# Moving x's transposes, the output projection and both layernorms to other units of the attention pipeline

## What is computed

```python
def layernorm(x): return (x - mean(x)) / sqrt(var(x) + 1e-5)

def attention(h):                      # 32 heads of 16 channels
    q, k, v = h @ Wq.T + bq, h @ Wk.T + bk, h @ Wv.T + bv
    q, k = apply_rope(q), apply_rope(k)          # q * cos + rotate_half(q) * sin
    scores = q @ k.T / sqrt(16)                  # causal mask, softmax over keys
    return softmax(where(causal, scores, -inf)) @ v @ Wo.T + bo

x = x + layernorm(attention(layernorm(x)))
x = x + layernorm(ffn(layernorm(x)))             # silu(x @ gate.T) * (x @ up.T) @ down.T
```

## Time and profile before

| | |
|---|---|
| median of three runs | 2859.64 us |
| profiled execution | 2851.13 us, its span 2849.4 us |
| TensorE matmul busy | 2545.8 us, 89% |
| VectorE busy | 2134.7 us, 75% |
| ScalarE busy | 1422.9 us, 50% |
| GpSimd busy | 1007.2 us, 35% |
| mean granted TensorE clock | 0.962 |
| attention phase | to about 1825 us of the span |

### The profile page before, as it was taken

How to read it: one execution, slowest core, us unless ns; L and a number is a source line. 1 busy time by engine, 2 the same in 40 slices (tenths; PEclk the granted TensorE clock), 3 DMA queues, 4 the chain that set the end, 5 groups by cost and what they waited for, 6 DMA issues and landing times. The chain is left out here.

```text
span 2849.4 us, 55752 instructions
## 1 busy us (share of the span) xinstructions
PE 2545.8 (89%) x19584; PEld 1220.5 (43%) x19584; DVE 2134.7 (75%) x6399; ACT 1422.9 (50%) x1838; POOL 1007.2 (35%) x1083
## 2 busy tenths in 40 slices
PE   4899889889898898898898997349999999999997
PEld 2444344444444443453444443114444444444443
DVE  6899889889889898898898997355455555555454
ACT  3666667666666666666666666142222222222221
POOL 4556455455455555564554563100000000000000
PEclk9999999999999999999999999669999999999999
DMA  5332332332332332333333331401111111111111
GB/s 170 94 89 76 113 111 68 113 120 66 111 117 71 108 113 73 108 101 88 111 91 91 104 104 32 197 18 45 44 59 44 69 49 44 59 44 74 44 44 45
DMA packets 125311, 236.64 MB, mean 83 GB/s; under 512 B 11440, under 2 KB 94896, under 8 KB 111920
## 3 DMA queue, kind: packets, MB, share of 16 engines
q1 hardware_dynamic: 123056, 232.84, 26.1%
q10 hardware_dynamic: 2048, 1.05, 0.1%
HBM read 148.39 MB, written 84.41 MB: 82 GB/s over the span
## 5 line engine op out<-in xcount | busy, mean ns | idle before, releaser
L650 DVE CUSTOM_DVE_ANT_0 mx<-mx,causal 128x512 f32<-128x512 f32 (+3 forms) x2048 | 944.7, 516 | 38.0 <-PE mx L779 34.7
L487 ACT ACTIVATE probs<-ts,exp_scale 128x1024 f32<-128x1024 f32 x640 | 709.5, 1109 | 421.8 <-PE ts L793 421.2
L1222 DVE SCALAR_TENSOR_TENSOR hidden<-gu,up_scale,silu 128x512 f32<-128x512 f32 x176 | 131.9, 749 | 418.7 <-PE gu L1272 418.7
L1081 ACT ACTIVATE silu<-gu,gate_scale 128x512 f32<-128x512 f32 x176 | 121.0, 688 | 632.0 <-PE gu L1272 632.0
L401 POOL TENSOR_SCALAR_AFFINE_SELECT probs<-probs 128x512 f32<-128x512 f32 x512 | 313.8, 637 | 199.9 <-ACT probs L487 199.8
L1056 POOL TENSOR_TENSOR f_rstd<-f_var,f_neg_half 128x4 f32<-128x4 f32 x32 | 32.3, 1010 | 929.6 <-DVE f_var L1199 647.2
L380 POOL TENSOR_TENSOR turned<-biased,sin_sb 64x512 f32<-64x512 f32 x128 | 172.0, 1344 | 469.5 <-ACT biased L472 469.5
L807 PE MATMUL xb<-probs,vs 128*32 128x512 f32 (+3 forms) x4096 | 308.7, 443 | 7.6 <-ACT shift_rows L493 5.6
L1270 PE MATMUL gu<-f_xT_hi,gate_hi 128*128 128x512 f16 x704 | 267.9, 381 | 52.1 <-issue 52.1
L779 PE MATMUL mx<-kT,qT 64*128 64x512 f16 (+3 forms) x2048 | 253.3, 306 | 37.8 <-DVE row_max L650 35.7
L650 DVE DVE_READ_ACCUMULATOR2_ANT row_max<- 128x1 f32 x2048 | 282.6, 138 | 0.0
(11 more groups left out here) (148 smaller groups left out, 4553.3 us busy)
## 6 DMA issues: line engine op xcount, KB each, us to landing
slots<-half SPq DMA_DIRECT2D x260, 128.0 KB, 12.5
qT<-slots SPq DMA_DIRECT2D x128, 256.0 KB, 3.8
kT<-slots SPq DMA_DIRECT2D x128, 256.0 KB, 4.0
xn<-x SPq DMA_DIRECT2D x16, 1024.0 KB, 6.8
xr<-x SPq DMA_DIRECT2D x16, 1024.0 KB, 4.9
slots<-half SPq DMA_DIRECT2D x256, 64.0 KB
x<-xr SPq DMA_DIRECT2D x16, 1024.0 KB, 5.6
f_xn<-x SPq DMA_DIRECT2D x16, 1024.0 KB, 4.8
```

Source lines behind the costliest of these rows:

```text
L487: nc.scalar.activation(probs[:, g % 2, u, :, :], ts[:, :, :], ACT.Exp, scale=exp_scale[:, 0:1]).then_inc(ts_read, 1)
L650: last = nc.vector.tensor_tensor_reduce(out=scores, in0=scores, in1=causal[:, T - P * (qt + 1):T], scale=1.0, scalar=-3e38, op0=ALU.add, o ...
```

## The change

- `TURNED`: x is transposed in groups 0, 1, 4, 6 (tiles 2, 3 of the next sequence, tiles 0, 1 of the one after), the attention output in groups 2, 3, 5, 7. Before it was x in 0, 2, 4, 6 and the attention output in 1, 3, 5, 7.
- `V_OR_OUT`: the output projection of the previous sequence in groups 3 to 6 instead of 1 to 4, v in groups 0, 1, 2 and 7 instead of 0, 5, 6, 7.
- First layernorm: load of x in unit 8, statistics in 14 and 15, variance in 15, root in 16, normalisation in 19, 20, 20, 21. Second: statistics in 21, 26, 31, 36, variance and root in 36; normalisation in 0, 1, 4, 5 and residual in 1 and 6 of the body after. x1 is stored in unit 9 of that body and xr loaded in unit 14.
- `cosine` stands behind the low half and the maxima in VectorE's list. As the low half is in unit 3 and the cosine product in unit 2, what changes is that unit 2's maxima come first.
- `aT_hi` and `aT_lo` have NC + 2 tiles. Every engine gets a `body(NB + 1)`; SP and GpSimd write out `body(1)` and loop from 2.

```diff
-        aT_hi = sb("aT_hi", [P, NC + 1, T], F16)
-        aT_lo = sb("aT_lo", [P, NC + 1, T], F16)
+        aT_hi = sb("aT_hi", [P, NC + 2, T], F16)
+        aT_lo = sb("aT_lo", [P, NC + 2, T], F16)
...
-        V_OR_OUT = (("v", 3, 0), ("out", 0, -1), ("out", 1, -1), ("out", 2, -1), ("out", 3, -1),
-                    ("v", 0, 1), ("v", 1, 1), ("v", 2, 1))
-        TURNED = (("x", 3, 1), ("a", 3, -1), ("x", 0, 2), ("a", 0, 0), ("x", 1, 2), ("a", 1, 0), ("x", 2, 2), ("a", 2, 0))
+        V_OR_OUT = (("v", 1, 0), ("v", 2, 0), ("v", 3, 0), ("out", 0, -1), ("out", 1, -1), ("out", 2, -1), ("out", 3, -1),
+                    ("v", 0, 1))
+        TURNED = (("x", 2, 1), ("x", 3, 1), ("a", 3, -1), ("a", 0, 0), ("x", 0, 2), ("a", 1, 0), ("x", 1, 2), ("a", 2, 0))
...
-        STATISTICS_AT = {5: (0, 1), 6: (2, 3)}
-        VARIANCE_AT = 6
-        ROOT_AT = 8
-        NORMALISE_AT = {10: (0, 1), 11: (2, 3)}
-        STATISTICS1_AT = {11: 0, 16: 1, 21: 2, 26: 3}
-        VARIANCE1_AT = 26
-        ROOT1_AT = 28
-        NORMALISE1_AT = {30: (0, 1), 31: (2, 3)}
-        RESIDUAL_AT = {31: (0, 1), 35: (2, 3)}
+        STATISTICS_AT = {14: (0, 1), 15: (2, 3)}
+        VARIANCE_AT = 15
+        ROOT_AT = 16
+        NORMALISE_AT = {19: (0,), 20: (1, 2), 21: (3,)}
+        STATISTICS1_AT = {21: 0, 26: 1, 31: 2, 36: 3}
+        VARIANCE1_AT = 36
+        ROOT1_AT = 36
+        NORMALISE1_AT = {0: (0,), 1: (1,), 4: (2,), 5: (3,)}
+        RESIDUAL_AT = {1: (0, 1), 6: (2, 3)}
...
-                    if s == 3 and exists(i + 2):
+                    if s == 8 and exists(i + 2):
                         sp.wait_ge(xT_full, NC * (i + 2))
                         sp.dma_start(xn[:, :, :], x[i + 2, :, :, :]).then_inc(x_in, 16)
-                    if s == 38 and exists(i - 1):
-                        sp.wait_ge(x1_ready, NT * i)
-                        sp.dma_start(x1[i - 1, :, :, :], xr[:, :, :]).then_inc(x1_out, 16)
-                    if s == 39 and exists(i - 1) and exists(i):
-                        sp.wait_ge(x1_out, 16 * i)
-                        sp.dma_start(xr[:, :, :], x[i, :, :, :]).then_inc(xr_in, 16)
+                    if s == 9 and exists(i - 2):
+                        sp.wait_ge(x1_ready, NT * (i - 1))
+                        sp.dma_start(x1[i - 2, :, :, :], xr[:, :, :]).then_inc(x1_out, 16)
+                    if s == 14 and exists(i - 2) and exists(i - 1):
+                        sp.wait_ge(x1_out, 16 * (i - 1))
+                        sp.dma_start(xr[:, :, :], x[i - 1, :, :, :]).then_inc(xr_in, 16)
...
-                    if u == 2:
-                        n, owner = QUERIES_KEYS[g]
-                        if exists(i + owner):
-                            cosine(i + owner, n)
                     if u == 3:
                         kind, c, owner = TURNED[g]
                         if in_turn(kind, i + owner):
...
                         maxima(i + ahead, n)
                         if n % NU == NU - 1:
                             shift_of_maxima(i + ahead, n // NU)
+                    if u == 2:
+                        n, owner = QUERIES_KEYS[g]
+                        if exists(i + owner):
+                            cosine(i + owner, n)
```

More of the change, by code:

```diff
@@ L328, in body @@
                         fetch_slots(i + owner, n)
-                    if s == 3 and exists(i + 2):
+                    if s == 8 and exists(i + 2):
                         sp.wait_ge(xT_full, NC * (i + 2))
                         sp.dma_start(xn[:, :, :], x[i + 2, :, :, :]).then_inc(x_in, 16)
-                    if s == 38 and exists(i - 1):
-                        sp.wait_ge(x1_ready, NT * i)
-                        sp.dma_start(x1[i - 1, :, :, :], xr[:, :, :]).then_inc(x1_out, 16)
-                    if s == 39 and exists(i - 1) and exists(i):
-                        sp.wait_ge(x1_out, 16 * i)
-                        sp.dma_start(xr[:, :, :], x[i, :, :, :]).then_inc(xr_in, 16)
+                    if s == 9 and exists(i - 2):
[4 more added lines that the diff above has]
+                        sp.dma_start(xr[:, :, :], x[i - 1, :, :, :]).then_inc(xr_in, 16)
             body(-1)
             body(0)
-            with sp.Fori(1, NB - 2) as i:
+            body(1)
+            with sp.Fori(2, NB - 2) as i:
                 body(i)
@@ L345, in _ @@
             body(NB)
+            body(NB + 1)
             sp.wait_ge(x1_out, 16 * NB)
@@ L429, in body @@
                                               minus_mean1[:, :], offset1[:, :], offset1_ready)
-                    if exists(i - 1):
+                    if exists(i - 2):
                         for t in RESIDUAL_AT.get(s, ()):
-                            before = residual(i - 1, t)
+                            before = residual(i - 2, t)
             inverse_root(0, var_ready, var[:, :], rstd[:, :], rstd_ready,
@@ L439, in _ @@
             body(0, (roped_done, 6))
-            with pool.Fori(1, NB - 2) as i:
+            body(1)
+            with pool.Fori(2, NB - 2) as i:
                 body(i)
@@ L453, in high_of_attention @@
                 act.wait_ge(aT_full, NC * i + c + 1)
-                nc.scalar.activation(aT_hi[:, (NC * i + c) % (NC + 1), :], xb[:, bank, :], ACT.Copy).then_inc(aT_hi_done, 1)
+                nc.scalar.activation(aT_hi[:, (NC * i + c) % (NC + 2), :], xb[:, bank, :], ACT.Copy).then_inc(aT_hi_done, 1)
             def normalise_x(i, t):
@@ L529, in body @@
                             normalise_x(i + 2, t)
-                    if exists(i - 1):
+                    if exists(i - 2):
                         for t in NORMALISE1_AT.get(s, ()):
-                            normalise_projected(i - 1, t)
+                            normalise_projected(i - 2, t)
             for t in range(NT):
@@ L619, in low_of_attention @@
                 dve.wait_ge(aT_hi_done, NC * i + c + 1)
-                place = (NC * i + c) % (NC + 1)
+                place = (NC * i + c) % (NC + 2)
                 nc.vector.tensor_tensor(aT_lo[:, place, :], xb[:, bank, :], aT_hi[:, place, :],
@@ L877, in project_out @@
                 for c in (2 * part, 2 * part + 1):
-                    place = (NC * seq + c) % (NC + 1)
+                    place = (NC * seq + c) % (NC + 2)
                     last = three_products(out, aT_hi[:, place, cols], aT_lo[:, place, cols], w_hi[:, 3, c, :], w_lo[:, 3, c, :],
```

## The result

The changed kernel takes 2744.84 us (median of four runs, 2744.56 to 2745.20). Run on the same chip, the kernel before takes 2861.89 (four runs, 2857.48 to 2865.51). The ratio is 0.9592, 95% interval 0.9575 to 0.9608: faster by 117 us, where 92 was forecast.

A forecast was written before the change was run, and what follows sets the result against it. TensorE and VectorE nearly fill regular groups; 11 us of each 109.25 us sequence are stalls. Sequences become 102.15, saving 85 over twelve; with neighbouring sequences and ends −92, so 2859.64 becomes about 2767, range 2722 to 2822.

The forecast's parts named there:

- Load and statistics of x: Group 1: with x loaded earlier, VectorE's 5.26 us wait, the idle time and slow clock go, 8.2 us per sequence.
- fourth rival: The x1 store behind the load makes x land after 16 us, VectorE waits again: 2830 to 2860 us; chance 0.06.
- Cosine product late: Regular groups: cosine product behind unit 2's maxima waits for GpSimd's second half, low half at +3.99; cost 0.
- Group 3: Statistics and variance of x ahead of its rotation delay the low half to +5.74: cost 1.45 per sequence, 2.8 if late.
- second rival: In group 3 the cosine product misses its gap and the clock falls: 2785 to 2835 us; chance 0.24.
- Normalisation of x: Group 4: four normalisations on ScalarE make the bias 1.12 us late, in place of the former 1.53.
- Second layernorm: Group 0 loses 0.32 instead of 1.53 to a normalisation; group 7 newly loses 1.06 to the root before its rotation.
- +4.29: Latest low-half start after a group's start that does not stall TensorE, which wants the freed bank at +5.03.
- SP and the ends: Moved x1 store, xr load and exchanged groups: 0 in regular groups; start −4 (−8 to 0), end −1 (−4 to +3).
- The offset of 8.5 us: The profiled execution of the kernel before lay 8.5 under the median; the same was expected for the changed kernel.
- the layernorms cost nothing: First rival: VectorE has room, so stretched layernorms add near 0; sequences 98.5 to 100, 2710 to 2742 us; chance 0.15.
- the other two: Rivals: low half stalls TensorE in every group, 2860 to 2900 (0.05); x still lands late, 2830 to 2860 (0.06).

The follow-up runs named there:

- e1: The kernel before without the load of x for sequences 2 to 15 (the layernorm works on what the tile holds): 2775.03 us, ratio 0.9696.
- e2: The kernel before with only the cosine product moved behind unit 2's maxima: 2857.29 us, ratio 0.9993.
- e3: The changed kernel with the cosine product back in front of unit 2's maxima: 2743.92 us, ratio 0.9588.
- e8: The changed kernel with variance and root of x moved from units 15 and 16 to unit 18: 2744.25 us, ratio 0.9587.
- e9: e6 with the load of x's separate statistics tile issued before the fetch of q or k instead of after it: 2717.05 us, ratio 0.9505.
- e4: The changed kernel with both inverse roots two units later (18 and 38), behind the rotation in GpSimd's list: 2764.54 us, ratio 0.9661.
- e10: e7 with the cosine product back in front of unit 2's maxima: 2728.10 us, ratio 0.9536.
- e5: The changed kernel with x's normalisation in units 18, 18, 19, 20 instead of 19, 20, 20, 21: 2735.43 us, ratio 0.9557.
- e7: e5 with the second layernorm's normalisations in units 3, 3, 4, 5 and residuals in 4 and 6: 2728.14 us, ratio 0.9532.
- e11: e9 with the second of x's four statistics in unit 8 instead of 6: 2714.35 us, ratio 0.9501.
- e6: e7 with one statistic of x per group, from a separately loaded tile, and SP's loop over bodies written out: 2743.18 us, ratio 0.9581.

## Why the prediction was right, and where not

Forecast 2767 in a range of 2722 to 2822, measured 2744.84. The sign and the main mechanism hold; the gain was 25 us larger than forecast, and the near agreement of the twelve sequences (85 forecast, 94 measured) holds errors both ways. Point by point:

1. **Load and statistics of x (−8.2 a sequence).** Right: group 1 takes 12.31 at a clock of 1.00, and the median of e1 falls by 85 us with the transfer alone. The fourth rival's mechanism, the x1 store behind the load, is seen in small: the median landing of x rose from 6.8 to 9.1. The longest, 9.7, was no longer than the 10.1 that the text reckoned with, and in the tightest sequence (body 11) x landed 4.5 before VectorE reached its statistics. The instructions on xn, in the changed kernel:

```profile
DMA to landing us min/median/max: 4.8/9.1/9.7
```

2. **Cosine product late (0).** Right: it starts at +2.36 and lasts 1.69 in a v group, low half at +3.98 against +3.99 worked out; e2 and e3 confirm the zero for regular groups.
3. **Group 3 (13.7).** Right at 13.77, low half at +5.81 against +5.74. The path was right too: VectorE's own lateness sets the low half. It reaches the cosine product at +5.20, 0.12 before GpSimd's first half ends, and gets in (body 4, from 524.45, VectorE and then GpSimd):

```profile
529.65 0.69 DVE L632 TENSOR_TENSOR roped<-biased,cos_sb 128x512 f32<-128x512 f32 x1
530.26 0.68 DVE L626 TENSOR_TENSOR aT_lo<-xb,aT_hi 128x512 f16<-128x512 f32 x1
...
528.50 1.27 POOL L382 TENSOR_TENSOR turned<-biased,sin_sb 64x512 f32<-64x512 f32 x1 [0.16 <-POOL offset L374]
529.85 1.61 POOL L384 TENSOR_TENSOR turned<-biased,sin_sb 64x512 f32<-64x512 f32 x1
```

By e8 and e9 the bunched statistics are the cost; the root's place in front costs next to nothing (e4 was worse without it). The lost race of the second rival, "It decides at 0.08 us", was seen in this group in one of thirteen sequences. There, in body 8, an idle time that the profile ascribes to issue pushes VectorE back by 0.3 us, while GpSimd keeps its time. VectorE, then GpSimd:

```profile
931.52 0.70 DVE L655 CUSTOM_DVE_ANT_0 mx<-mx,causal 128x512 f32<-128x512 f32 x1 [0.23 <-issue]
...
934.31 1.68 DVE L632 TENSOR_TENSOR roped<-biased,cos_sb 128x512 f32<-128x512 f32 x1
935.91 0.68 DVE L626 TENSOR_TENSOR aT_lo<-xb,aT_hi 128x512 f16<-128x512 f32 x1
...
932.83 1.27 POOL L382 TENSOR_TENSOR turned<-biased,sin_sb 64x512 f32<-64x512 f32 x1 [0.16 <-POOL offset L374]
934.18 1.26 POOL L384 TENSOR_TENSOR turned<-biased,sin_sb 64x512 f32<-64x512 f32 x1
```

The cosine product comes 0.13 after the second half has begun and lasts 1.68 instead of 0.69. TensorE stands for 2.47, and its next products last 0.60 where they lasted 0.39: they run at 1.2 GHz, and the window's clock is 0.90.

```profile
936.65 0.39 PE L771 MATMUL xb<-w_hi,aT_hi 128*128 128x512 f16 x1 [2.47 <-DVE aT_lo L626]
...
937.31 0.60 PE L771 MATMUL xb<-w_hi,aT_hi 128*128 128x512 f16 x1
```

This is the second rival's mechanism, at 2.9 us once instead of thirteen times. With the cosine product in front the race is gone (e3 and e10 both show 0.69), but TensorE still stands 0.39 and 1.44 us in both. In e3 the clock stays at 1.00 (group of 14.05); in e10 it falls to 0.89 (15.65). Why the same idle times end differently was not settled. The rival's "up to 1.2 more each" for the clock has no row behind it; between e3 and e10 it is 1.6.

The race has a second place, which the text didn't have. In group 0 of body 4, from 486.53, VectorE reaches the cosine product at +3.53, where it is +3.25 in the other sequences, and so 0.03 after GpSimd's second half has begun (VectorE, then GpSimd):

```profile
490.06 1.78 DVE L632 TENSOR_TENSOR roped<-biased,cos_sb 128x512 f32<-128x512 f32 x1
...
490.03 1.26 POOL L384 TENSOR_TENSOR turned<-biased,sin_sb 64x512 f32<-64x512 f32 x1
```

The group takes 13.28 instead of 12.61; with the cosine product in front (e3) it takes 12.71.

4. **Normalisation of x (group 4 at 13.4).** Right: 13.27, TensorE waits 0.88 for the bias, and e5 removes it by moving it.
5. **Second layernorm (group 0 at 12.6, group 7 at 13.4).** The first half is right, 12.62 but for body 4, and e7 removes it. The second failed: group 7 takes 12.32. The step that failed is "with VectorE's cosine product waiting since +3.6". The rows of group 7, from 575.95, VectorE and then GpSimd:

```profile
577.88 0.17 DVE L700 TENSOR_SCALAR var<-mv 128x4 f32<-128x4 f32 x1
...
579.44 0.69 DVE L632 TENSOR_TENSOR roped<-biased,cos_sb 128x512 f32<-128x512 f32 x1
580.05 0.68 DVE L626 TENSOR_TENSOR aT_lo<-xb,aT_hi 128x512 f16<-128x512 f32 x1
...
578.13 1.02 POOL L372 TENSOR_TENSOR rstd<-var,neg_half 128x4 f32<-128x4 f32 x1 [5.47 <-DVE var L700]
579.23 0.20 POOL L374 TENSOR_TENSOR offset<-minus_mean,rstd 128x4 f32<-128x4 f32 x1
579.59 1.67 POOL L382 TENSOR_TENSOR turned<-biased,sin_sb 64x512 f32<-64x512 f32 x1 [0.16 <-POOL offset L374]
```

The variance ends at +2.1 and the root follows, both as worked out. By the text's own sum the first half would start at 4.88 less 1.27, +3.61, and VectorE reach its product at +3.6: a tie, which was read as lost. VectorE came at +3.49, 0.15 before GpSimd, and it was GpSimd's half that lasted longer (1.67). The low half at +4.10 is before +4.29, so 1.06 a sequence, 13 us in all, were not there. A tie should have stood in the sum as a race with two ends, as point 3's did.

6. **SP and the ends.** Regular groups kept their time: 0 was right. The start gave 2.0 (the first group begins 0.24 later, body 0 takes 95.39 instead of 97.60), against 4. The end gave 5.3, against 1 and outside its bound of 4: from the start of body 15 to the second phase it is 120.52 us instead of 125.12, and the second phase itself is 0.7 shorter. No experiment took the end apart, so what shortened it is open.

**The sum.** Bodies 2 to 13 gave 94.3 where 85 was forecast. Group 7 explains 13; against it stand the two lost races, 2.9 in group 3 of body 8 and 0.67 in group 0 of body 4. Body 1 gave 3.1 (2 forecast), the one after them 1.2 (0). The profiled span fell by 105.9, from 2849.4 to 2743.5.

**The offset of 8.5 us.** The medians differ by 117.1 and the profiles by 105.9: the other 11 are in "I expect the same for the changed kernel", the second step that failed. The profiled execution of before lay 10.8 under the median of 2861.89; that of after, 2745.2, lies on its own. The wait for x is a likely source, as groups 1 differ by 11 us in all between the one profiled execution of before and that of e2. No two executions of one kernel were profiled, so this is not shown. The change removes this wait, and its four runs lie within 0.6 us where before had 8. It isn't the only source of spread: e10, without the wait, ran from 2719.68 to 2734.01.

Of the rivals, the first (the layernorms cost nothing, 2710 to 2742) was nearest in time and wrong in mechanism for the changed kernel: groups 3 and 4 cost 2.6 a sequence. It describes e9 and e11.

**The range.** Its own chances don't add up to what it asks. With half of the first rival, a quarter of the second and all of the other two outside, 0.245 is left out, where no more than 0.2 was wanted.

## What to carry over

An idle time that one late transfer opens can cost more than its length: here 5.26 us of waiting made 6.75 (20.47 less the 13.72 of e1), through work that piles up behind it and the clock. The statistics' own 1.5 only moved. Where VectorE is full, put small extra steps one to a group, and look at each step's neighbours in every queue, SP's above all: e6 lost to one place in SP's list what e9 gained. Where two engines that lock each other out arrive within 0.2 us, write the sum down with both ends, and don't count on removing a wait as a gain: it may be what keeps a short operation out of a long one's way.

## What the runs showed of the hardware

- A VectorE `tensor_scalar` of 128x4 is held by a GpSimd operation of 64x512 for all of its time: 1.27 us instead of 0.17 (e4).
- In body 8's group 3, VectorE idles 0.23 us with issue as the cause, before the same maxima in the changed kernel, e3, e5, e7 and e10. So it belongs to the program and not to chance. In e6, e9 and e11, whose statistics lie elsewhere, 0.16 us of the same kind stand before the variance in that group. What causes it no run shows.
- TensorE idle for 0.39 and 1.44 us in the same places of the same group kept a clock of 1.00 in e3 and fell to 0.89 in e10.
